# Toeplitz rows of two heads in one transfer, an earlier turn of the probabilities, and a weight split moved: one block of a transformer on one core

## The reference

```
kernel[h, l] = 2 * Re(sum_n Cs[h, n] * exp(dtA[h, n] * l))   # h: 64 step-heads, l: 1024 features
y  = causal_convolution(x * mask, kernel) + x * mask * D     # along the 1024 features, per head h
q, k, v = (y * mask) @ Wq.T, @ Wk.T, @ Wv.T                  # 32 query heads, 8 key heads of 32
attn = softmax(rope(q) @ rope(k).T / sqrt(32) + causal)      # 64 x 64 per head and sequence
x1 = x + (attn @ v) @ Wo.T
c  = einsum("bct,bcd->bdt", x1, weights[condition])          # channel mixing
out = x1 + c @ W_base.T + moe_lora(c)                        # 8 experts of rank 8, top 2
```

## Time and profile before

| | us |
|---|---|
| median of 3 runs (903.91 to 904.40) | 904.31 |
| the profiled execution | 903.88 |
| its span | 902.0 |
| PE busy | 877.8 (97%) |
| DVE busy | 436.1 (48%) |
| POOL busy | 400.0 (44%) |
| ACT busy | 202.6 (22%) |

### The profile page before, as it was taken

How to read it: one execution, slowest core, us unless ns; L and a number is a source line. 1 busy time by engine, 2 the same in 40 slices (tenths; PEclk the granted TensorE clock), 3 DMA queues, 4 the chain that set the end, 5 groups by cost and what they waited for, 6 DMA issues and landing times.

```text
span 902.0 us, 24817 instructions
## 1 busy us (share of the span) xinstructions
PE 877.8 (97%) x10982; PEld 764.5 (85%) x10982; DVE 436.1 (48%) x917; ACT 202.6 (22%) x366; POOL 400.0 (44%) x309
## 2 busy tenths in 40 slices
PE   2999999999999999999999999999999999999998
PEld 2999999988888888887777777777789999999997
DVE  6565551111222222269887777788534433334444
ACT  4455542100000000033222222233331101111010
POOL 3444564203555556569977888777511000000000
PEclk9999999999999999999999999999999999999999
DMA  3788778112224222265544454543452121221201
GB/s 82 195 218 223 190 196 188 60 47 70 71 70 105 70 71 71 55 191 163 146 139 129 159 170 144 160 150 114 162 165 79 48 94 72 72 77 66 94 25 71
DMA packets 83402, 105.35 MB, mean 117 GB/s; under 512 B 41696, under 2 KB 54880, under 8 KB 83296
## 3 DMA queue, kind: packets, MB, share of 16 engines
q1 hardware_dynamic: 80304, 102.73, 38.5%
q10 hardware_dynamic: 2480, 0.51, 0.3%
q0 software_dynamic: 512, 0.53, 0.2%
HBM read 74.08 MB, written 29.65 MB: 115 GB/s over the span
## 4 chain that ended last, share of the span: by engine, by line
PE 89%; POOL 4%; DVE 3%; DMA 2%; issue 1%; SPq 0%; ACT 0%; DVEq 0%; POOLq 0%
PE ps L1329 21%; PE ps L1139 20%; PE ps L867 19%; PE ps L569 10%; PE ps L831 5%; PE ps L580 5%; PE ps L1095 3%; PE ps L1075 2%; PE ps L1302 2%; POOL rf L978 1%; PE ps L1352 1%; POOL rot L974 1%; DMA raw_cols<-in_dram 1%; PE ps L1353 1%; POOL sc L1166 1%
## 5 line engine op out<-in xcount | busy, mean ns | idle before, releaser
L1329 PE MATMUL ps<-wb,xf 128*128 128x420 f32 (+1 forms) x1152 | 195.8, 330 | 0.0
L1329 PEld LDWEIGHTS ps<-wb,xf 128*128 128x128 f32 x1152 | 188.3, 188 | 2.8 <-issue 0.2
L867 PE MATMUL ps<-y_hi,w_hi 128*128 128x512 f32 x320 | 125.1, 391 | 0.0
L867 PE MATMUL ps<-y_hi,w_lo 128*128 128x512 f32 x320 | 124.6, 389 | 0.0
L867 PE MATMUL ps<-y_lo,w_hi 128*128 128x512 f32 x320 | 124.6, 389 | 0.0
L1139 PE MATMUL ps<-y_hi 128*128 128x512 f32 x256 | 103.0, 402 | 0.9 <-POOL y_lo L1002 0.9
L1139 PE MATMUL ps<-y_hi,y_lo 128*128 128x512 f32 x256 | 100.2, 391 | 0.0
L1139 PE MATMUL ps<-y_lo,y_hi 128*128 128x512 f32 x256 | 100.2, 391 | 0.0
L569 PE MATMUL ps<-xc,toep 64*128 64x192 f32 (+4 forms) x1088 | 96.7, 330 | 1.5 <-DVE ym L654 0.6
L569 PEld LDWEIGHTS ps<-xc,toep 64*128 64x128 f32 x1088 | 91.0, 187 | 4.5 <-issue 2.2
L974 POOL TENSOR_TENSOR rot<-rot,cst 128x512 f32<-128x512 f32 x40 | 53.7, 1343 | 72.8 <-DVE rot L945 72.8
(11 more groups left out here) (153 smaller groups left out, 1260.6 us busy)
## 6 DMA issues: line engine op xcount, KB each, us to landing
toep<-kpad SPq DMA_DIRECT2D x62, 272.0 KB, 4.9
xc<-in_dram SPq DMA_DIRECT2D x32, 256.0 KB, 4.2
q_rows<-rf SPq DMA_DIRECT2D x32, 256.0 KB, 2.8
q<-q_rows SPq DMA_DIRECT2D x16, 512.0 KB, 4.0
xr<-in_dram SPq DMA_DIRECT2D x16, 512.0 KB, 4.4
x_scratch<-xr SPq DMA_DIRECT2D x16, 512.0 KB, 2.6
x<-x_scratch SPq DMA_DIRECT2D x16, 512.0 KB, 3.5
out_dram<-x SPq DMA_DIRECT2D x15, 512.0 KB, 2.6
```

Of the source, the lines that this page charges most:

```text
L867: mm = pe.matmul(kq_bank(n), w[a][:, j, :], yt[b][:, j, g * 512:(g + 1) * 512], start=(j == 0 and a + b == 0), stop=(j == NJ - 1 and a == 1))
L1329: mm = pe.matmul(joint_bank(i, piece)[:, 0:hi - lo], xf[i % 2][:, a, t, :], wb[t][:, w4_place(t, c), lo:hi], start=(t == 0 and a + c == 0) ...
```

## The change

Three edits. The Toeplitz rows of both heads of a pair are read by one transfer over all 128 partitions, and the columns are cut in two halves of 544, so that there are two transfers a pair as before. The DRAM side of each is a pattern of three dimensions: 2 heads, 64 shifts, 544 columns. The first pair's rows are loaded as before. `rows_landed` gives the count for PE's wait; with two halves it is 32 for each use of a slot, as before. In a step of the attention DVE turns the probabilities right after the scale and takes the maximum after o_lo. And POOL makes the last low part of `wo` ahead of the fifth subtraction instead of after the last rotary tile.

```diff
+        ROW_HALVES = [(0, (L + HALF) // 2), ((L + HALF) // 2, L + HALF)]
+
+        def rows_landed(n):
+
+            earlier = n // TR
+            whole = 16 * len(ROW_HALVES)
+            return whole * (earlier + 1) if n % TR else 16 * 2 + whole * earlier
...
         def load_toeplitz(sp, n):
             if n - TR + 1 > 0:
                 sp.wait_ge(pe_conv, n - TR + 1)
-            for r in range(2):
-                load_rows(sp, n, r, 0, L + HALF, ld_toep[n % TR])
+            for lo, hi in ROW_HALVES:
+                sp.dma_start(toep[:, n % TR, lo:hi],
+                             bass.AP(kpad, head(n, 0) * (KROW + 1) + lo, [[GP * (KROW + 1), 2], [1, HALF], [1, hi - lo]]))\
+                  .then_inc(ld_toep[n % TR], 16)
...
             else:
-                pe.wait_ge(ld_toep[n % TR], 16 * 2 * (n // TR + 1))
+                pe.wait_ge(ld_toep[n % TR], rows_landed(n))
...
                 if lead == 6:
+                    wo_lo(gp, 7)
                     subtract_max(gp, 4)
...
-            wo_lo(gp, 7)
...
                 if w + CR < NUNIT:
                     scale(v, w + CR)
-                    maximum(v, w + CR)
+                if w + 1 < NUNIT:
+                    turn_probs(v, w + 1)
                 if w < NUNIT:
                     o_lo(v, w)
-                if w + 1 < NUNIT:
-                    turn_probs(v, w + 1)
+                if w + CR < NUNIT:
+                    maximum(v, w + CR)
                 if w + 2 < NUNIT:
                     sums(v, w + 2)
```

## The result

The changed kernel takes 1153.03 us (median of four runs, 1152.52 to 1154.25), the kernel before 904.11 us in the same comparison: ratio 1.275, 95% interval 1.2734 to 1.2765. The forecast was 1146 us. The profiled execution has a span of 1152.4 us, against 902.0.

The account below looks back on a forecast made before the run. TensorE, busy 877.8 of 902.0 us, bounds the kernel; two DMA engines would bind the convolution. 903.9 + 242.3 - 1.2 = 1145.0, against the median 1145.4, rounded up to 1146 us; range 1100 to 1226.

Parts of the forecast that it names:

- Two engines instead of sixteen: Convolution's Toeplitz loads: the leading count of 2 in DRAM puts each new transfer on two DMA engines, not 16.
- 11.37 us a pair at 24.5 GB/s: Convolution: each of two engines moves 278.5 KB a pair at 24.5 GB/s, 11.37 us against 4.37 us of matmuls.
- the 26.7 us counted for other traffic: Convolution, same two engines: x tiles 18.7 us, wraw loads 4.0, kernel stores and instruction fetches 4.
- The far end of 15.3 GB/s: Convolution: two engines at the crowded rate of 15.3 GB/s each, total 1371 us; chance 0.03.
- The clock priced at zero: Convolution: PE idling 7 us or more a pair costs 0 us of clock; at worst the last pair's extra 4.4 us.
- The 240 us of waits named as the sign: Convolution: PE's waits would be headed by some 240 us for toep.
- the 242.3 forecast: Convolution: the stage ends at 407.5 us instead of 165.16, 242.3 us lost.
- The turn at 0 us: Attention step on VectorE: turning probabilities earlier raises slack from 1.3 to 3.1 us, all covered, gain 0 us.
- The remainder at 1.2 us: First projection: the earlier last weight remainder on POOL removes PE's wait whole, gain 1.2 us.
- Late next: After the remainder's move: normalise(4) ends 0.9 us after the moved turn would take it, within a slack of over 3.
- The rival of 16 engines: Convolution: new transfers spread over 16 engines, 902.0 to 903.1 us; chance 0.11, split 0.06 faster, 0.05 the same.
- The point from which it was to decide: Convolution: the 16-engine rival decides once a pair's rows take under 4.37 us, needing 5.2 engines or more.

Follow-up runs that it names:

- the series of outermost counts: Changed kernel with later pairs' rows read from one kernel row, in 2, 4, 8 or 16 groups of shifts: 1152.47, 984.36, 918.28, 909.70 us.
- turn_only: Kernel before with the second edit alone (probabilities turned right after the scale): 903.14 us, ratio 0.998.
- outer16: Changed kernel with later pairs' rows read from one kernel row as 16 groups of 8 shifts: 909.70 us, ratio 1.004.
- shift128: Changed kernel with later pairs' rows read from one kernel row as one run of 128 shifts: 906.09 us, ratio 1.003.
- outer4: Changed kernel with later pairs' rows read from one kernel row as 4 groups of 32 shifts: 984.36 us, ratio 1.088.

## Why the prediction was right, step by step

**Two engines instead of sixteen: right**, by the share of 0.13, by the 868 small packets and by the series of outermost counts.

**11.37 us a pair at 24.5 GB/s: right within 3%.** The last rows landed at 412.5 us instead of 403.1. Issued from 22.2 us on, with 1.5 us for the landing and the 26.7 us counted for other traffic, the rows took 362 us instead of 352, that is 23.8 GB/s an engine, an estimate that rests on those two counts. The far end of 15.3 GB/s played no part: two engines made 23 to 25 in the short stretches. The row for 24.5 was misread, without harm. From 651 to 652 us the kernel before moved these packets:

```profile
DMA packets 103, 0.38 MB, mean 381 GB/s; under 512 B 10, under 2 KB 10, under 8 KB 103
```

The 93 large ones carry 4.1 KB each, so most are x rows of 4096 B and not the weights' 2192 B. The weights follow, from 653 to 655 us, at 23.9 GB/s, closer still to what was measured.

**The clock priced at zero: wrong by 1.5 us.** It fell: the two short stretches above show 0.50 (1.2 GHz) and 1.00 (2.4 GHz), the stage's mean is 0.75. The last pair took 418.4 - 412.5 = 5.9 us instead of 4.4, the others hid it. That lies between the 0 taken and the 4.4 named as the worst. The 240 us of waits named as the sign came as 186 us of waits and 68 us of slower matmuls. The Trainium skill (TensorE: Matmul & The Clock Gate, Part 1) has the clock fall in idle stretches, and here it agrees with the trace. The row that spoke for zero, the clock after the first 15.8 us, said nothing of gaps inside the work.

These two, 9.4 and 1.5 us, make all but 0.1 of the 11.0 us by which the convolution lost more than the 242.3 forecast.

**The turn at 0 us: wrong by about 1.6 us.** The rest of the kernel came out 2.8 us shorter, and 1.2 of these were forecast, for the remainder. The slack moved as worked out. In turn_only, a settled step:

```profile
467.30 1.22 DVE L1157 SCALAR_TENSOR_TENSOR sc<-ps,causal 128x1024 f32<-128x1024 f32 x1 [1.21 <-PE ps L1075]
...
468.55 1.25 DVE L1186 STREAM_TRANSPOSE pt<-sc 128x1024 f32<-128x1024 f32 x1
...
472.86 0.94 PE L1095 MATMUL ps<-pt,vc 32*32 32x128 f32 x48
```

The turn ends at 469.80, 3.1 us ahead of the values, where it was 1.3. Nobody needed that slack, and most of the gain came from elsewhere: the two pauses of the score matmuls under "issue", a row of the same list that was read past because it named no releaser.

**The remainder at 1.2 us: right.** In the changed kernel, POOL and PE around the first projection, whose first matmul starts at 689.16:

```profile
687.10 2.36 POOL L1012 TENSOR_TENSOR y_lo<-raw_cols,y_hi 128x1024 fp32r<-128x1024 f32 x1
...
689.42 2.88 POOL L1176 TENSOR_TENSOR sc<-sc,stat 128x1024 f32<-128x1024 f32 x1
...
694.83 0.94 PE L1105 MATMUL ps<-pt,vc 32*32 32x128 f32 x48
```

The remainder ends at 689.5, long before its matmul; the projection takes 694.83 - 689.16 = 5.67 us instead of 6.87, against 5.65 forecast. Late next was, as forecast, the turn after it, which waits for normalise:

```profile
698.69 1.25 DVE L1196 STREAM_TRANSPOSE pt<-sc 128x1024 f32<-128x1024 f32 x1 [0.82 <-POOL sc L1190]
```

0.82 us, against 0.9 worked out, and the values follow at 702.21, 2.3 us after it ends.

**The rival of 16 engines: its price was wrong.** It was put at 902 to 903 us from a rate of 24.5 GB/s an engine into 128 partitions. That rate was read from x rows and weights, whose rows lie apart, in a stretch without other traffic. With windows of one kernel row the engines made 13.0 to 13.6, and outer16 and shift128 took 910 and 906 us. Had the real transfer been spread and behaved like these two, the rival would have had the sign wrong. The point from which it was to decide, 5.2 engines, was wrong too: eight engines still cost 13 us. The verdict rests on two engines being the case, so these errors didn't touch it.

## What to carry to other kernels

Look at both sides of every transfer before merging two into one: here the outermost count in DRAM, against 128 partitions, decided how many of the 16 engines carried it, and a leading 2 made two of them do all the work. A falling DMA share beside new waits on transfers is the mark of this, and the count of packets under 512 B proves it. A rate taken from one transfer holds for another only if destination and source are alike: here, in packets of 2176 B in the convolution's traffic, an engine moved 18.5 GB/s into all partitions from rows that lay apart and 13 to 14 from windows of one row; into half of the partitions, in packets of 4352 B, it was 15.5.

## What the runs showed of the hardware that was not expected

Sixteen engines reading shifted windows of one DRAM row into 128 partitions, in packets of 2176 B, moved 13.0 and 13.6 GB/s each; the same packets from 128 rows 4 KB apart 18.5. Packets of 4352 B from one row reached 15.7. And while transfers that only two engines carry were queued, SP was held up: its Toeplitz issues grew from a median of 0.6 us to 5.3 us, x tiles and weights for all engines behind them. With four engines (outer4) the median was still 0.55 us.
